# Tile pass: eight places for loaded tiles, the store ahead of the load on SyncE's queue, the expert number read one piece ahead, a row's four sums spread over four steps

## The reference, cut to what matters

```python
def step(acc, ew):
    w_gu, w_d, cw = ew              # [352, 256], [256, 176], weight of this expert for each token
    h = _silu_mul(x @ w_gu.T, I)    # silu(gate) * up, I = 176
    return (acc + h @ w_d.T * cw[:, None], None)
...
return (shared + sparse).reshape(orig_shape)
```

## Time and profile before

| | |
|---|---|
| runs (3) | 738.62, 739.25, 745.31 us, median 739.25 |
| profiled execution | 737.96 us, span 736.1 us |
| outside the span | 1.86 us |
| granted TensorE clock, mean | 0.960 |
| PE, DVE, ACT, POOL busy | 82%, 68%, 58%, 53% |
| DMA moved | 78.93 MB, mean 107 GB/s |
| first tile transposed | at 454.08 us |
| last tile's store issued | just before 719.80 us |

### The profile page before, as it was taken

One profiled execution on the slowest core, in us unless ns is written; L12 is line 12 of the kernel. 1 busy time (PEld: TensorE's weight loads), 2 busy tenths in 40 slices (PEclk: granted clock), 3 DMA queues, 4 the chain that ended last, 5 costly groups with the idle time before them and its releaser, 6 DMA issues.

```text
span 736.1 us, 18487 instructions
## 1 busy us (share of the span) xinstructions
PE 603.2 (82%) x5880; PEld 470.1 (64%) x5880; DVE 500.2 (68%) x1518; ACT 423.9 (58%) x1060; POOL 393.6 (53%) x437
## 2 busy tenths in 40 slices
PE   0578899999999999999999885887777776776770
PEld 0257788988898889888988763555545544444540
DVE  4347798989888989988768674555455555565562
ACT  3477887788668877786677331544434434444440
POOL 0126768888888887788878772000224233233233
PEclk9788999999999999999999997999999999999995
DMA  6734323342343234221001112222334444455343
GB/s 203 247 100 144 105 92 108 122 127 86 109 120 112 75 108 146 86 81 52 18 28 45 37 61 91 73 86 87 108 118 148 130 137 133 126 151 150 109 125 105
DMA packets 55679, 78.93 MB, mean 107 GB/s; under 512 B 7330, under 2 KB 46370, under 8 KB 55588
## 3 DMA queue, kind: packets, MB, share of 16 engines
q1 hardware_dynamic: 48676, 58.87, 25.8%
q0 software_dynamic: 6912, 18.88, 8.3%
HBM read 44.43 MB, written 33.29 MB: 106 GB/s over the span
## 4 chain that ended last, share of the span: by engine, by line
PE 61%; DMA 16%; issue 8%; POOL 5%; DVE 4%; ACT 3%; SPq 2%; POOLq 0%; DVEq 0%; ACTq 0%
DMA toeplitz_hi<-x_slots 13%; PE ps L637 8%; PE ps L719 7%; PE ps L534 6%; PE ps L567 5%; PE ps L468 5%; PE ps L659 4%; PE ps L522 3%; PE ps L587 3%; PE ps L571 3%; PE ps L710 2%; PE ps L505 2%; PE ps L495 2%; PE ps L739 2%; POOL kv_lo L1408 2%
## 5 line engine op out<-in xcount | busy, mean ns | idle before, releaser
L1475 POOL DMA_INDIRECT toeplitz_lo<-y_slots,slots x64 | 61.3, 958 | 98.7 <-DMA y_slots<-stage 80.1
L719 PE MATMUL ps<-w_gate_up_hi,toeplitz_hi 128*128 x316 | 88.3, 327 | 19.7 <-issue 18.0
L1408 POOL TENSOR_TENSOR kv_lo<-kv,kv_hi 128x512 f16<-128x512 f32 x64 | 79.4, 1241 | 32.7 <-ACT kv_hi L852 32.5
L1447 POOL DMA_INDIRECT x_slots<-x_norm,slots x64 | 69.2, 1081 | 20.6 <-issue 14.5
L1396 POOL TENSOR_TENSOR kv<-ctx_t_sb,v_t 128x512 f32<-128x512 f32 x64 | 69.1, 1089 | 15.9 <-ACT v_t L841 15.7
L710 PE MATMUL ps<-identity,toeplitz_hi 128*128 128x128 f32 x158 | 35.2, 307 | 48.9 <-DMA toeplitz_hi<-x_slots 47.6
L821 ACT ACTIVATE probs<-ps,row_neg_max 128x128 f32<-128x128 f32 x256 | 71.6, 392 | 2.1 <-DVE row_neg_max L1023 2.0
L1318 DVE TENSOR_TENSOR toeplitz_hi<-ps,toeplitz_hi 128x256 f16<-128x256 f32 x79 | 33.3, 423 | 56.3 <-ACT toeplitz_hi L934 56.3
L1472 POOL DMA_DIRECT2D stage<-shared_sum x16 | 9.3, 580 | 109.6 <-DVE stage L1347 69.5
L940 ACT ACTIVATE stage<-ps 128x176 f32<-128x176 f32 x79 | 25.0, 317 | 73.7 <-PE ps L719 73.7
L1323 DVE SCALAR_TENSOR_TENSOR stage<-stage,ps 128x176 f32<-128x176 f32 x79 | 26.5, 336 | 58.2 <-ACT stage L940 58.2
(11 more groups left out here) (218 smaller groups left out, 2202.7 us busy)
## 6 DMA issues: line engine op xcount, KB each, us to landing
stage<-in_w_units SPq DMA_DIRECT2D x36, 512.0 KB, 3.8
toeplitz_hi<-x_slots SPq DMA_DIRECT2D x79, 128.0 KB, 2.3
y_slots<-stage SPq DMA_DIRECT2D x79, 128.0 KB, 1.7
x_slots<-zeros SPq DMA_DIRECT2D x15, 512.0 KB
x_slots<-zeros SPq DMA_DIRECT2D x1, 2432.0 KB
x_sb<-in_x SPq DMA_DIRECT2D x16, 128.0 KB, 2.2
ctx_t_sb<-in_ctx_in SPq DMA_DIRECT2D x16, 128.0 KB, 3.6
shared_sum<-x_shared SPq DMA_DIRECT2D x16, 128.0 KB, 1.7
```

The costliest lines, as they stand in the source:

```text
L719: last = nc.tensor.matmul(psum[2 + t % 2][:, 0:2 * INTER], bxT[a][t % 2][:, kc, :], egu[b][:, bass.ds(e, 1), kc, :].rearrange("p a n -> p ...
L1408: nc.gpsimd.tensor_tensor(flat(kvh[1][g % 2]), kv[g % 2][:].rearrange("p h j i -> p (h j i)"), flat(kvh[0][g % 2]), ALU.subtract).then_inc ...
L1447: pool.indirect_dma_start(out=xbuf, out_offset=bass.IndirectOffsetOnAxis(ap=slots[:, row, j:j + 1], axis=0), in_=xn[2][row % 2][:], in_off ...
L1475: pool.indirect_dma_start(out=yg[n][j], out_offset=None, in_=ybuf[0:(last_tile(row) + 1) * P], in_offset=bass.IndirectOffsetOnAxis(ap=slot ...
```

## The change

There are eight places for loaded tiles instead of four. Places 4 to 7 are the four buffers of the convolution's split products (`kv_hi`, `kv_lo`), which nothing uses in this stage. On SyncE's queue the store of tile `t` now stands ahead of the load, which is of tile `t + 8`. TensorE reads the expert number of tile `s` in step `s` behind `gate_up(s-1)`, and not at the start of `gate_up(s)`. One of three transposes in `turn_inner` is left out: it wrote the same place as the second. The four sums of a row are spread over four steps, one in each, and begin at `last_tile(row) + 10`; the row's store stands at `t = combine_at(row) + 4`. `gather` on GpSimd is not changed.

```diff
+NX = 8
...
-        xg = [t_hi[:, n * E:(n + 1) * E] for n in range(4)]
+        products_mem = [kv_part[n][:].rearrange("p g c n -> p (g c n)").bitcast(F32) for kv_part in kvh for n in range(2)]
+        xg = [t_hi[:, n * E:(n + 1) * E] for n in range(4)] + products_mem
...
             def load_tile(t):
-                t_xT.wait(sp, t - 4)
-                sp.dma_start(xg[t % 4], xbuf[t * P:(t + 1) * P, :]).then_inc(s_xg[t % 4], 16)
+                t_xT.wait(sp, t - NX)
+                sp.dma_start(xg[t % NX], xbuf[t * P:(t + 1) * P, :]).then_inc(s_xg[t % NX], 16)
...
-            for t in range(4):
+            for t in range(NX):
                 load_tile(t)
             for t in range(TILES):
-                if t + 4 < TILES:
-                    load_tile(t + 4)
                 store_tile(t)
+                if t + NX < TILES:
+                    load_tile(t + NX)
                 if store_at(t) is not None:
                     store_row(store_at(t))
...
             def gate_up(t):
                 t_xlo.wait(pe, t)
                 t_inner.wait(pe, t - 2)
-                experts[t] = e = pe.value_load(table[0:1, t:t + 1], min_val=0, max_val=EXPERTS - 1)
+                e = experts[t]
...
-                nc.tensor.transpose(to[:, 0:P], h[:, 0:P], id_sb[:])
                 for c in range(2):
...
                     if 0 <= s - behind < TILES:
                         piece(s - behind)
+                    if piece is gate_up and s < TILES:
+                        experts[s] = pe.value_load(table[0:1, s:s + 1], min_val=0, max_val=EXPERTS - 1)
...
-            def combine(row):
+            def combine(row, j):
                 n = row % 2
-                dve.wait_ge(s_acc[n], 16 * (row // 2 + 1))
-                dve.wait_ge(s_yg[n], 16 * TOP * (row // 2 + 1))
-                for j in range(TOP):
-                    if j > 0:
-                        combined.wait(dve, row, j)
-                    nc.vector.scalar_tensor_tensor(out=acc[n], in0=yg[n][j], scalar=cw4[:, row, j:j + 1], in1=acc[n],
-                                                   op0=ALU.mult, op1=ALU.add).then_inc(combined.sem, 1)
+                if j == 0:
+                    dve.wait_ge(s_acc[n], 16 * (row // 2 + 1))
+                    dve.wait_ge(s_yg[n], 16 * TOP * (row // 2 + 1))
+                else:
+                    combined.wait(dve, row, j)
+                nc.vector.scalar_tensor_tensor(out=acc[n], in0=yg[n][j], scalar=cw4[:, row, j:j + 1], in1=acc[n],
+                                               op0=ALU.mult, op1=ALU.add).then_inc(combined.sem, 1)
...
                 for row in range(NB):
-                    if combine_at(row) == s:
-                        combine(row)
+                    if 0 <= s - combine_at(row) < TOP:
+                        combine(row, s - combine_at(row))
             for row in range(NB):
-                if combine_at(row) >= TILES + 3:
-                    combine(row)
+                for j in range(TOP):
+                    if combine_at(row) + j >= TILES + 3:
+                        combine(row, j)
...
 def combine_at(row):
-    return last_tile(row) + 7
+    return last_tile(row) + 10
...
 def store_at(t):
-    return next((row for row in range(NB) if combine_at(row) + 1 == t), None)
+    return next((row for row in range(NB) if combine_at(row) + TOP == t), None)
```

More of the change, by code:

```diff
@@ L286, in build @@
         s_zero, s_clear = sem("zeros_set"), sem("slots_cleared")
-        s_xg = [sem(f"tile_loaded{i}") for i in range(4)]
+        s_xg = [sem(f"tile_loaded{i}") for i in range(NX)]
         s_ys = [sem(f"tile_stored{i}") for i in range(4)]
@@ L706, in turn_x @@
             def turn_x(t):
-                pe.wait_ge(s_xg[t % 4], 16 * (t // 4 + 1))
+                pe.wait_ge(s_xg[t % NX], 16 * (t // NX + 1))
                 t_xlo.wait(pe, t - 2)
                 for c in range(KC):
-                    last = nc.tensor.transpose(psum[t % 2][:, c * P:(c + 1) * P], xg[t % 4][:, c * P:(c + 1) * P], id_sb[:])
+                    last = nc.tensor.transpose(psum[t % 2][:, c * P:(c + 1) * P], xg[t % NX][:, c * P:(c + 1) * P], id_sb[:])
                 last.then_inc(t_xT.sem, 1)
```

## The result

| | before | after |
|---|---|---|
| median of the runs | 740.92 us (4 runs, 738.62 to 745.31) | 768.66 us (4 runs, 764.57 to 769.98) |
| profiled execution | 737.96 us, span 736.1 | 764.57 us, span 762.7 |
| granted TensorE clock, mean | 0.960 | 0.914 |

The changed kernel is slower: ratio 1.036, 95% interval 1.029 to 1.042. 767 us was forecast.

What follows compares the result with a forecast made beforehand. Late tile loads bound TensorE, with the gather loop nearly closed. y(78) at 740.2 plus 24.3 gave a 764.5 us span, 766.4 with the 1.86 around it; as the profiled execution lay below the median, 767, range 747 to 784.

Steps and rivals of the forecast that it cites:

- a step without waits: TensorE's unhindered step in the tile pass: 2.25 us less 0.11 for the dropped transpose, 2.14 us.
- y done to gathered data: SyncE's row store, GpSimd's start, its four gathers and the way to the sums: 0.84 + 2.37 + 5.83 + 1.90, 10.9 us.
- gathered data to the next such y: VectorE's sum and x_lo, two TensorE steps partly at low clock, and y_out: 7.5 us, bounds 5.8 and 8.4.
- a turn of the loop: Row store, gather, sums and next y, per four tiles: 18.5 us against 13.2 before, eleven times, 203.5 us.
- last y, to the end: After y(78), rows 12 to 15 are stored behind the loop: 24.3 us against 16.7 before.
- Loads, queue order: Tile loads on SyncE's queue, needed four steps after leaving, at least 8.5 us, are covered; otherwise 47.6 us of waits stay.
- Expert number: TensorE's read behind six queued matmuls costs nothing; bounds 0 and 0.52 us a step.
- The transpose: Leaving out one transpose on TensorE saves 0.11 us a step.
- First part: Tile pass from step 4 to step 36 at 2.14 us a step, ending at 531.9 instead of 567.21: 35 us gained.
- Sums and row stores: The store gather(row + 2) waits for leaves in the step VectorE wants its data: 11 waits from step 36, 203.5 us.
- The clock: TensorE's clock falls after 7.5 us idle each turn, returning 5 us after restart; staying up instead gives 748 us, 14%.
- rival A: The gather loop does not hold, gathered data come in time, all steps take 2.14 us: 657 us, chance 8%.

Runs made afterwards that it cites:

- best_four: three_store_early with four places for loaded tiles and the load ahead of the store again: 737.90 us, ratio 0.988.
- three_number_back: three_places with the expert number read at the start of gate_up again: 667.25 us.
- best_number: three_store_early with the expert number read at the start of gate_up again: 702.77 us, ratio 0.939.
- store_early: The changed kernel with a row's store four places earlier on SyncE's queue, at t = combine_at(row): 667.34 us, ratio 0.905.
- three_places: The changed kernel with three places instead of two for gathered rows and acc: 665.26 us, ratio 0.892.
- sums_at_7: The changed kernel with sums begun three steps earlier, at last_tile + 7, their store moving with them: 778.44 us, ratio 1.051.
- spread_only: The kernel before with only the spread sums, their later start and the change's store place: 803.56 us, ratio 1.091.
- warm: The changed kernel with 60 unused transposes on TensorE ahead of each gate_up that waits for sums of rows 2 to 12: 750.33 us, ratio 1.016.
- three_store_early: The changed kernel with three places for gathered rows and acc, and the row's store at t = combine_at(row): 646.89 us, ratio 0.872.
- sums_undone: The changed kernel with all four sums back in one step at last_tile + 7, store at combine_at + 1: 693.03 us, ratio 0.927.
- best_transpose: three_store_early with the third transpose in turn_inner put back: 696.49 us, ratio 0.932.

## Why the prediction was right

Step by step, as the forecast put it:

| step of the forecast | forecast | measured in the profile after |
|---|---|---|
| a step without waits | 2.14 us | 2.13 |
| start of step 36 | 531.9 us | 528.31 |
| y done to gathered data | 10.9 us | 11.2 (567.70 to 578.94), mean of eleven 11.2, from 10.2 to 12.5 |
| gathered data to the next such y | 7.5 us | 7.0 (578.94 to 585.93), mean of eleven 7.5, from 6.9 to 8.2 |
| a turn of the loop | 18.5 us | 18.80 |
| turns | 11 | 11 |
| y(76) to y(78) | 4.3 us | 2.7 |
| last y, to the end | 24.3 us | 24.8 |
| span | 764.5 us | 762.7 |

**Loads, queue order.** Right. TensorE waits for one tile only, the first. That the loads set the pace before is shown by `best_four`, where the wait returns.

**Expert number.** Right that it is hidden: `three_number_back` and the 2.13 us steps of `best_number`.

**The transpose.** Right, 0.11 us a step.

**First part.** The gain was 39 us instead of 35: 1.6 because the tile pass happened to begin at 452.49 and not 454.08, the rest because the first steps were shorter; the clock was back at 1.00 from 457 us on, where the forecast had kept's start, made with a clock at 0.50 until 461.

**Sums and row stores.** Right in place, count and size. `store_early` and `three_places` undo the dependence in two ways and the time falls by 101 and, against another group's runs, 103 us; `sums_at_7` moves both ends of it together and nothing is won; `spread_only` has it without the gain and is 63 us slower than before. The forecast did not name the second distance, from the last tile's store to the row's own sums, which `sums_at_7` shows; in the changed kernel it costs nothing.

**The clock.** Right: it falls in each pause, and `warm` measures its share as 1.9 us of a turn or a little more, where the forecast had 18.5 - 16.8 = 1.7. The time of its return, 5 us in the forecast, was 3 us in one turn and 5 in the next; the mean of the eleven came out as reckoned.

**The errors** nearly cancel. The start of step 36 is 3.6 us early and the last two steps are 1.6 us shorter; the eleven turns, from y(32) to y(76), take 206.4 us instead of 203.5, the excess being on the way from y to the gathered data, and the end is 0.5 us longer. Together that is the 1.8 us between a span of 764.5 and one of 762.7. The closeness of 767 to 768.66 is partly luck: the start of the tile pass alone moved by 6 us and more among the profiles, and the profiled execution lies 4.1 us below the median, where the forecast had added 1.3.

**Where a size was off**: not in the changed kernel but in what was worked out for the experiments. The 10.9 us from y to gathered data is a price beside a paused TensorE. Beside a full pace it is 13 us from the row's store alone, so `store_early` still loses 15 us in its steps. Had rival A come true by four steps of distance, 657 us would have been too low by 8 to 10 (`store_early`, `three_places`); with eight steps `three_store_early` goes below it, as its end is shorter too. And the deeper prefetch alone, with the old sums, gives the 693 us of `sums_undone`.

## What to carry to other kernels

When a store, a gather and a sum are linked by a shared buffer, count the steps between the point where the store leaves its queue and the point where the data are wanted, in each engine's written order: here the spread moved the store by three steps more than the sums, the distance fell from three steps to none, and the wait hid behind an edit that was meant to smooth the work. Check this distance again after any edit that speeds up the steps, because a margin counted in steps shrinks in microseconds. Here moving one store, or adding one more buffer, turned a loss of 28 us into a gain of 73 or 79, and the two together into one of 98. A margin can also be missing between a tile's store and the row's own sums, which no shared buffer links: count both.

## What was not expected of the hardware

- Latency under load: from the issue of a 128 KB output store to the start of the work that waits for it took 2.8 us on average (2.3 to 4.0) in the changed kernel, at 90 to 103 GB/s in windows of 50 us, and 3.9 us (2.5 to 5.3) in `store_early`, at 176 to 184 GB/s.
- 60 idle-time transposes in each of eleven pauses made the changed kernel 18 us faster, by keeping TensorE at 1.00 in ten of them.
- In one group of runs ScalarE and VectorE stood still together for 2 us and more at a time, 31 us within 120 in `best_transpose`, for nothing that the profile shows, while the same steps in another group had 0.8 us of it. Every such wait of over 0.8 us began while GpSimd issued gathers. Its cause is open.
